# Inverse roots of queries' and keys' sums of squares: from GpSimd's power to ScalarE's logarithm and exponential, in both transformers of a four-layer network

## What is computed

```python
q, k, v = split(x @ Wqkv)                         # per head of 64
q = q / maximum(norm(q), 1e-12) * q_scale         # the inverse root is here
k = k / maximum(norm(k), 1e-12) * k_scale         # and here
q = q*cos*scale + rotate_half(q)*sin*scale        # k likewise, by 1/scale
attn = softmax(where(mask, 8 * q @ k.T, -max))    # windows of 32 or 64 keys
x = x + (attn @ v) @ Wo
x = x + (a * gelu(gate)) @ W2 + b2                # a, gate = split(ln(x) @ W1 + b1)
```

## Time and profile before

| | us |
|---|---|
| median of three runs | 4103.28 |
| the three runs | 4100.12, 4103.28, 4103.32 |
| span of the profiled execution | 4092.7 |
| PE busy | 3711.7 (91%) |
| DVE busy | 2873.0 (70%) |
| ACT busy | 2446.0 (60%) |
| POOL busy | 2308.6 (56%) |
| mean granted TensorE clock | 0.968 |

### The profile page before, as it was taken

The page is one execution under the profiler, slowest core; times in us unless marked ns, Lnnn a source line. Parts: engine busy times, 40 slices in busy tenths (PEclk is TensorE's granted clock), DMA queues, the critical chain, the costliest instruction groups (busy, mean ns, idle before and its releaser), DMA issues. The chain is left out here.

```text
span 4092.7 us, 101193 instructions
## 1 busy us (share of the span) xinstructions
PE 3711.7 (91%) x40365; PEld 2524.8 (62%) x40365; DVE 2873.0 (70%) x6494; ACT 2446.0 (60%) x4999; POOL 2308.6 (56%) x2227
## 2 busy tenths in 40 slices
PE   7986999997999979999999999999999998768886
PEld 5664555544666656666666666666666666646665
DVE  4436544403666568888888888888888887558885
ACT  2233555424455557767777777777776776447775
POOL 2003000001111268888888888888888886257773
PEclk9987999998899989999999999999999999889998
DMA  0000000100000021111112112112111111120000
GB/s 25 2 3 23 1 1 1 30 0 7 2 2 2 2 87 41 41 56 52 40 41 68 41 40 65 41 41 68 41 41 41 41 39 32 34 73 23 23 23 19
DMA packets 103249, 128.53 MB, mean 31 GB/s; under 512 B 38232, under 2 KB 55681, under 8 KB 101889
## 3 DMA queue, kind: packets, MB, share of 16 engines
q1 hardware_dynamic: 102784, 122.05, 11.1%
HBM read 31.95 MB, written 3.54 MB: 9 GB/s over the span
## 5 line engine op out<-in xcount | busy, mean ns | idle before, releaser
L404 POOL TENSOR_TENSOR t_inv<-t_ssq,half 128x8 f32<-128x8 f32 x448 | 780.3, 1745 | 83.6 <-DVE t_ssq L682 63.9
L455 PE MATMUL t_wa<-t_w_qkv,t_resid 128*128 128x512 f32 x1344 | 693.9, 616 | 42.7 <-DMA t_scales<-in_L_ffn_k_scale 38.8
L415 POOL TENSOR_TENSOR t_ra<-t_qn,t_rot 128x512 f32<-128x512 f32 x448 | 570.6, 1274 | 84.8 <-DVE t_qn L689 76.2
L606 ACT ACTIVATE t_p<-t_p 128x384 f32<-128x384 f32 (+1 forms) x448 | 240.9, 538 | 331.2 <-DVE t_p L706 322.4
L715 DVE TENSOR_TENSOR t_ra<-t_ra,t_rb 128x512 f32<-128x512 f32 x448 | 311.0, 716 | 121.6 <-POOL t_rb L417 121.2
L484 PEld LDWEIGHTS t_T<-ident,t_p 128*96 128x96 f32 (+1 forms) x1792 | 192.0, 128 | 312.6 <-ACT t_p L606 280.1
L416 POOL TENSOR_TENSOR t_rb<-t_qn,t_rot 128x256 f32<-128x256 f32 x448 | 367.6, 821 | 0.0
L417 POOL TENSOR_TENSOR t_rb<-t_qn,t_rot 128x256 f32<-128x256 f32 x448 | 335.8, 749 | 0.0
L680 DVE TENSOR_REDUCE t_ssq<-t_sq 128x8 f32<-128x512 f32 x448 | 304.8, 680 | 12.3 <-ACT t_sq L598 8.6
L455 PEld LDWEIGHTS t_wa<-t_w_qkv,t_resid 128*128 128x128 f32 x1344 | 212.8, 192 | 160.9 <-issue 130.4
L492 PE MATMUL t_T<-ident,t_ra 128*128 128x128 f32 x1792 | 268.5, 277 | 44.7 <-ACT t_gg L645 32.2
(11 more groups left out here) (420 smaller groups left out, 8367.7 us busy)
## 6 DMA issues: line engine op xcount, KB each, us to landing
t_v<-t_vn SPq DMA_DIRECT2D x192, 198.0 KB, 2.6
t_v<-t_vn SPq DMA_DIRECT2D x248, 132.0 KB, 2.4
t_v<-t_vn SPq DMA_DIRECT2D x144, 66.0 KB, 1.9
t_w_qkv<-in_L_ffn_Wqkv SPq DMA_DIRECT2D x6, 1536.0 KB, 6.7
t_v<-t_nothing SPq DMA_DIRECT2D x48, 66.0 KB, 1.9
t_w_o<-in_L_ffn_Wo SPq DMA_DIRECT2D x6, 512.0 KB
f_h<-t_L_ffn_h_w SPq DMA_DIRECT2D x2, 1024.0 KB, 8.0
t_w<-in_L_ffn_W SPq DMA_DIRECT2D x6, 341.0 KB
```

The costliest lines, as they stand in the source:

```text
L404: pool.tensor_tensor(inv[:, n % 2, r, :], ssq[:, n % 2, r, :], g["half"][:, 0:8], ALU.pow).then_inc(inved.sem, 1)
L415: pool.tensor_tensor(ra[:, n % 2, r], qn[:, r], spread(cos, 1, 8), ALU.mult).then_inc(cosd.sem, 1)
L455: pe.matmul(bank, resid[:, b, lo:lo + P], w_qkv[:, l % 2, at:at + 512], start=True, stop=True).then_inc(wa_up.sem, 1)
```

## The change

GpSimd no longer computes `inv`. ScalarE does, for q and k together (16 columns): a natural logarithm of `ssq` scaled by 2^16, and then the exponential of -0.5 times that. Both stand behind the copies to `kT`, and in a slot with a feed-forward behind the second table switch as well. VectorE's product takes the factor 2^8 that the scaling calls for, and is a three-operand instruction with the broadcast `inv` as its first operand; q's product now waits for the roots of q and of k. The two activations on `spare` are gone: the table sets are loaded by instructions of their own, and the set that is loaded behind the Gelu has both the logarithm and the exponential.

```diff
         ssq = st.sb("ssq", [P, 2, 2, 8])
+        logs = st.sb("logs", [P, 2, 2, 8])
...
-                    if ahead is not None:
-                        n = ahead
-                        for r in range(2):
-                            pool.wait_ge(floored.sem, floored.at(n, r + 1))
-                            pool.tensor_tensor(inv[:, n % 2, r, :], ssq[:, n % 2, r, :], g["half"][:, 0:8], ALU.pow).then_inc(inved.sem, 1)
...
+                def roots(n):
+                    act.wait_ge(floored.sem, floored.at(n, 2))
+                    act.activation(logs[:, n % 2], ssq[:, n % 2], ACT.Ln, scale=LIFT).then_inc(logged.sem, 1)
+                    act.wait_ge(logged.sem, logged.at(n))
+                    act.activation(inv[:, n % 2], logs[:, n % 2], ACT.Exp, scale=-0.5).then_inc(inved.sem, 1)
+
+                act.preload_act_table_set("natural_log_exp_and_others")
...
-                        act.activation(spare[:, 0:1], g["half"][0:1, 0:1], ACT.Gelu)
+                        act.preload_act_table_set("gelu_and_others")
...
                     if ffn is not None:
-                        act.activation(spare[:, 1:2], g["half"][0:1, 0:1], ACT.Exp)
+                        act.preload_act_table_set("natural_log_exp_and_others")
+                    if ahead is not None:
+                        roots(ahead)
                     if ahead is not None and ffn is not None:
                         copy_v(ahead)
...
-                    v.wait_ge(inved.sem, inved.at(n, r + 1))
+                    v.wait_ge(inved.sem, inved.at(n))
...
-                    v.tensor_tensor(qn[:, r], wa[:, wa_job[kind, n] % 3, :].rearrange("p (h d) -> p h d", h=8),
-                                    spread(inv[:, n % 2, r, :], 2, HD), ALU.mult).then_inc(normed.sem, 1)
+                    v.scalar_tensor_tensor(out=qn[:, r], in0=spread(inv[:, n % 2, r, :], 2, HD), scalar=LIFT ** 0.5,
+                                           in1=wa[:, wa_job[kind, n] % 3, :].rearrange("p (h d) -> p h d", h=8),
+                                           op0=ALU.mult, op1=ALU.mult).then_inc(normed.sem, 1)
```

More of the change, by code:

```diff
@@ L217, in transformer @@
     xnT, u, ident, identb = g["xnT"], g["u"], g["ident"], g["identb"]
+    LIFT = 2.0 ** 16
     tile_of = lambda G: G // NG
@@ L283, in transformer @@
         lnT = st.sb("lnT", [P, P])
-        spare = st.sb("spare", [1, 2])
         gg = st.sb("gg", [P, NH, P])
@@ L306, in transformer @@
         floored = st.event("floored", 2)
-        inved = st.event("inved", 2)
+        logged = st.event("logged")
+        inved = st.event("inved")
         normed = st.event("normed", 2)
@@ L408, in _ @@
                     if ahead is not None:
+                        n = ahead
                         t = tile_of(n)
```

## The result

The change makes the kernel slower: 4443.05 us median (4440.28 to 4443.94, four runs) against 4101.7 (four runs), a ratio of 1.0835 with a 95% interval of 1.082 to 1.085. The prediction was 4422, within 4345 to 4510. The profiled execution's span grew from 4092.7 to 4441.9, by 349.2.

A forecast was written before the change was run, and what follows sets the result against it. DVE was taken to set the pace at projection slot ends, with POOL's powers off the path. First transformer 242, second 53 and clock 24 us made 319, span 4411.7; with 10.6 around it 4422, range 4345 to 4510.

The forecast's parts named there:

- The powers are worth nothing: POOL's 448 powers are off the path; removing them can directly give at most DVE's 4.6 us of waits.
- The rival that POOL was the hidden limit: Not slower: freeing POOL removes DVE's 1.38 us rotation wait in 95 tiles, 131 us back, near 3972; chance 0.04.
- The roots: On ACT, 0.22 us each with 0.03 per hand-over, 0.50 us from first root to DVE's product.
- The products: DVE's products by inv become three-operand instructions, 0.07 us longer each; bounds 0 and that.
- The projection slot's end: First transformer: DVE's product starts 0.59 us later; with longer products, ln and the maximum are 0.73 late.
- The feed-forward slot's end: First transformer: roots stand behind the table load, so the next slot's first maximum starts 1.93 us later.
- The rival of absorption: Part of the delay is absorbed: one 1.93 us delay per tile, no clock dip, 236 us, about 4340; chance 0.13.
- The second transformer's wait: At its slot ends ln comes 1.71 us later, nothing hiding it: 31 intervals, 53 us.
- The clock: Second transformer: PE's longer gap makes half the slots dip, 1.57 us each, 24 us; bounds 0 and 49.
- The table load's drain: On ACT: the skill has 1.38 us on top of each 1.28 us load; the prediction saw no drain.
- the rival built on such a wait: ACT waits 1.28 us more before each root behind a switch: 161 us more, near 4583; chance 0.03.
- The activation on one element: Ahead of the Gelu on ACT; its removal saves 0.11 us per tile of the first transformer.

The follow-up runs named there:

- e12_early_q_first: Changed kernel with table switch and roots moved earlier on ScalarE, in feed-forward slots behind the Gelu with qT's copy between load and roots: 4123.91 us, 1.0061 times the kernel before.
- e6_proj_only: Changed kernel, but in the first transformer roots on ScalarE only in slots without a feed-forward, GpSimd's power in the others: 4266.57 us, 1.0408 times the kernel before.
- e5_ff_only: Changed kernel, but in the first transformer roots on ScalarE only in slots with a feed-forward, GpSimd's power in the others: 4393.3 us, 1.0716 times the kernel before.
- e7_loads_only: Kernel before the change, with only the activations on one element replaced by table-load instructions of their own: 4095.12 us, 0.9991 times the kernel before.

## Why the prediction was right

**The powers are worth nothing.** Shown. POOL lost 772 us of work, and with the roots placed as well as they were here, in `e12_early_q_first`, the kernel is still 0.6% slower than before. DVE's wait for the rotation, on which the rival rested, did not shrink: 123 us in all, from 121. The rival that POOL was the hidden limit is out.

**The roots.** 0.22 us each and 0.03 to the next, as taken.

**The products.** Taken 0.07 us longer each, from the nearest three-operand row (0.749); they take 0.684, against 0.683. The row was of another line with other operands. This part of the sum, 0.27 us a tile or 26 us, was nothing.

**The projection slot's end.** Predicted 0.73, measured 0.58 on the timeline and 0.48 as the mean of a tile in `e6_proj_only`.

**The feed-forward slot's end.** Predicted 1.93, measured 1.89, and 1.86 in `e5_ff_only`. That is close partly by luck: 0.14 of the 1.93 are the longer products, which did not come, and 0.10 of gaps between the instructions were missing. The first transformer came to 220 us, predicted 242. The 22 are 26 for the products and 14 for what the tile means lack against the timeline, less 9 for the gaps and 10 for the activation on one element (below), to a rounding. The rival of absorption is out: the two delays add up to within 0.02 us, and all that is hidden is the 0.3 us of every fourth tile. DVE's short maximum did get shorter with less of POOL beside it, 0.172 us in the median from 0.204, but from a feed-forward slot's first maximum to its last `kT` copy the time is 8.36 us (2020.83 to 2029.19), from 8.38 (2006.01 to 2014.39).

**The second transformer's wait.** Predicted 1.71 a slot, measured 1.57 with the clock kept up (1.76 in the slots of full length), 49 us instead of 53.

**The clock.** This is the term that was mis-sized: 24 us predicted, 31 x 2.21 = 69 measured, outside the 0 to 49 that I had given for it. Two things were wrong in it. The clock fell in every slot, not in half of them, and that cost 2.21 us each, not the 1.57 of the single dip in the earlier trace rows, for the stretch at 1.2 GHz was 6.8 us long and not 3.4. The slots were 16.37 us apart for that reason, outside the 14.3 to 15.9 forecast. The prediction also has the old dip begin while PE stood waiting, but the windows show it 0.4 us after PE had gone on. In the first transformer the clock did not fall, as forecast: 1.00 from 1600 to 3400 us, before and after.

**What was left out.** 12 us around the counted intervals, taken as nothing. With them the parts are 220 + 49 + 69 + 12 = 350, against 349.2 of span.

**Luck in the sum.** The forecast was 319 us of span. Two terms were too high, by 22 and 4 us, and two too low, by 45 and 12. The path was right, but that the span came out 30 us off (4441.9 against 4411.7), where the two low terms alone make 57, is owed to misses of opposite signs.

**The table load's drain.** ACT's first root stands 0.01 us behind the end of the load in the changed kernel (2006.83 + 1.28, then 2008.12). The Trainium skill (ScalarE: Activation LUTs, section What ACT_TABLE_LOAD costs) has a drain of 1.38 us on top of the load; the trace shows none in this place either, and the rival built on such a wait is out.

**The activation on one element.** I had counted its 0.11 us as a gain in every tile of the first transformer, 10 us, and not at all in the second. It was the other way round. In the changed kernel the load does stand that much closer to the Gelu, but DVE waited for the Gelu only 29 times in the whole kernel, 22 us in all, no more often than the 32 slots of the second transformer, and in the feed-forward slot that follows the timeline above DVE's product (2027.34) starts straight behind its own queue. Alone, in `e7_loads_only`, the 0.1 us counted in the second transformer and not in the first.

## What to carry to other kernels

The share of busy time said that POOL had 780 us to give; the line of waits for its result said 4.6. When work is moved to another engine, look for the instruction that waits for its result and ask when the new producer comes to it in its own order, since half a microsecond of work behind three copies and a table load made the slot 1.9 us longer. A wait that is made longer on TensorE can be priced twice, once by itself and once by the clock: it was in the second transformer, and not in the first. A gain that is hidden can become one when the wait beside it goes: measure small edits together as well as apart.

## What was not expected of the hardware

With PE's gap at the slot's end grown from 1.12 to 3.01 us the granted clock did not dip now and then but in slot after slot of the second transformer, 0.80 on average for some 500 us, and such a dip was twice as long as the one in the kernel before. Twenty more 128-column matmul instructions in each gap, 2.40 us of them, kept it at 1.00. A three-operand product from PSUM with a broadcast first operand took 0.684 us, one of the same size at another line 0.749.
